# Expert rows added into out by accumulating scatters, gates made per group of rows

## The chip, the cores and the metric

One core of a Trainium2 chip runs the kernel. The engines are TensorE (PE), VectorE (DVE), ScalarE (ACT), GpSimd (POOL) and SyncE (SP); 16 DMA engines move data between HBM and the on-chip memories SBUF and PSUM. The metric is the device time of one execution in microseconds.

## The reference

x has 16 x 256 rows of 128 floats: T = 4096 rows, 32 tiles of 128. The first half is attention without softmax, which the kernel computes through small products per batch. The second half is a mixture of 8 experts, two for each row:

```
x = x + attention(layernorm(x)) @ Wo + bo       # 16 heads of 8, q and k of unit length
z = layernorm(x)
topk_w, topk_idx = top_k(softmax(z @ Wg.T), 2)
eo[e] = gelu(z @ w1[e] + b1[e]) @ w2[e] + b2[e]         # 128 -> 512 -> 128, erf gelu
x = x + sum over the two chosen experts of topk_w * eo[idx]
```

## The kernel before

T = 4096 rows are 8 groups (NG) of 4 tiles (G) of 128 rows. Each engine runs one program written out in order; they meet in semaphores.

**Attention stage.** All engines go through the same steps n of STEPS, each step working on several groups at different depths, in the order that the loop of each engine lists. For a group g: DVE takes statistics of x (stats_of_x, moments, squared, variance), ACT the root (deviation), DVE inverts (scale_and_shift), ACT makes xn (normalised), TensorE turns and projects it (turn_x, project), ACT squares q and k (squares), DVE sums (sums_of_squares), bounds (bounded), ACT takes the root (norms), DVE inverts (inverse_norms) and scales q and k (unit_qk). TensorE makes the rest of the attention (keys_of_x to attend). DVE adds it to x2, the rows after attention, which stay in SBUF (attended), finds the two largest logits and their experts (largest, where_largest, chosen, either), and from a running count the place of each row in its expert's region of xs (places). ACT writes the normalised rows twice into row (rows); GpSimd scatters them to xs, a table in HBM with one region for each expert, by 8 indirect DMAs of 128 rows for each group (line 463): 64 in all. SP hands row and slot back (s_free) two groups later. The weights w1 and w2 are split on the way into a high and a low part (centred_w1, high_w1, low_w1, high_w2, low_w2). weights() on DVE prepares the attention's weights once, in step -1.

After the last group DVE makes the tables of the slots (slot_table), SP and ACT write zero rows behind each expert's rows (pads), and DVE and ACT make all gates at once from the kept logits (lines 1068 to 1078 and 765).

**Slots.** There are NS = 71 slots of 128 rows of one expert each. For each, SP loads the rows from xs (line 396), U = 8 loads ahead at most, held back by s_back; TensorE turns them, multiplies by w1 in three products (lines 630 to 632), turns h and multiplies by w2 (lines 649 and 652); ACT does Gelu and the high parts, DVE the low parts (lines 1083 and 1088) and y (result, result_high, lines 1095 and 1100). GpSimd scatters y to ys (put, line 471), a table in HBM with a row for each of the two choices of each input row. The target row comes with the row from xs; rows of padding have a target outside of ys and are left out.

**Combining.** SP loads the two rows for each input row back from ys, group by group (line 405), DVE and ACT multiply by the gates and add to x2, ACT's queue writes out (lines 801 and 803).

## Time and profile before

| | us |
|---|---|
| median of 3 runs (323.61 to 323.96) | 323.89 |
| the profiled execution | 324.12 |
| its span, first to last instruction | 322.2 |

| engine | busy us | share of the span |
|---|---|---|
| PE | 254.3 | 79% |
| DVE | 208.9 | 65% |
| ACT | 170.3 | 53% |
| POOL | 149.9 | 47% |

The span in 40 slices of 8 us; a digit is the busy share in tenths, PEclk the granted TensorE clock, and DMA the mean busy share of the DMA engines:

```profile
PE   3847999998879530789999999999999999994000
PEld 1636777677558300269998999899899989893000
DVE  3474999799999679036556556655665666563475
ACT  4244566686754443055655655565565556551353
POOL 4380037757777778404443444444344444444000
PEclk9999997899995655699999999999999999999555
DMA  3798001111111114121221222222212222210996
```

The first 16 slices are the attention stage, then come the slots, and the last three are the combining stage. In the profile a name such as "ring<-xs" is output<-input, a group of instructions is named by its line in the kernel, "[0.30 <-issue]" is the idle time before an instruction and what ended it, and the time of a DMA "to landing" runs from its issue to the arrival of its semaphore.

### The profile page before, as it was taken

The page shows a single profiled execution, that of the slowest core. Times are in us where ns is not written, and L with a number is a line of the kernel's source. Part 1 is how long each engine was busy: PE and PEld are TensorE (multiplying, and loading weights), DVE is VectorE, ACT ScalarE, POOL GpSimd, SP SyncE. Part 2 cuts the span into 40 slices and gives each one's busy share as a digit, 9 for nine tenths or more (in the row PEclk, how much of TensorE's full clock was granted, in tenths as well). Part 3 has the DMA queues.
Part 4 walks back from the last instruction along what each step waited for, and adds up shares of the span by engine and source line. Part 5 has one row for each costly group of instructions (what it writes and reads, how often), then busy time and mean ns, then how long its engine had stood idle before and what let it go on. Part 6 is the DMA issues. An engine that isn't in the chain of part 4 may idle for free.

```text
span 322.2 us, 6689 instructions
## 1 busy us (share of the span) xinstructions
PE 254.3 (79%) x1611; PEld 211.2 (66%) x1611; DVE 208.9 (65%) x788; ACT 170.3 (53%) x392; POOL 149.9 (47%) x172
## 2 busy tenths in 40 slices
PE   3847999998879530789999999999999999994000
PEld 1636777677558300269998999899899989893000
DVE  3474999799999679036556556655665666563475
ACT  4244566686754443055655655565565556551353
POOL 4380037757777778404443444444344444444000
PEclk9999997899995655699999999999999999999555
DMA  3798001111111114121221222222212222210996
GB/s 86 219 356 238 2 16 50 58 36 57 52 49 49 50 49 100 51 50 51 57 68 53 59 67 66 60 55 67 65 48 67 63 59 60 63 43 1 257 337 188
DMA packets 33643, 27.60 MB, mean 86 GB/s; under 512 B 4395, under 2 KB 28601, under 8 KB 33607
## 3 DMA queue, kind: packets, MB, share of 16 engines
q1 hardware_dynamic: 24344, 16.39, 18.7%
q0 software_dynamic: 4320, 8.43, 7.9%
q10 hardware_dynamic: 4944, 2.36, 2.6%
q8 instruction: 16, 0.26, 0.4%
q14 instruction: 19, 0.16, 0.2%
HBM read 16.05 MB, written 11.57 MB: 86 GB/s over the span
## 4 chain that ended last, share of the span: by engine, by line
PE 55%; POOL 15%; DVE 10%; issue 7%; DMA 6%; ACT 3%; SPq 2%; DVEq 0%; POOLq 0%; ACTq 0%
POOL xs L463 15%; PE psQK L630 6%; PE psG L649 5%; PE psQK L632 5%; PE psQK L631 5%; PE psQ L639 5%; PE psO L649 5%; PE psKV L639 5%; PE psG L652 4%; PE psO L652 4%; DMA w1s<-ys 4%; PE psQK L519 3%; DVE n L896 2%; PE psO L624 1%; PE psX L624 1%
## 5 line engine op out<-in xcount | busy, mean ns | idle before, releaser
L471 POOL DMA_INDIRECT ys<-ring x71 | 68.9, 970 | 94.4 <-DVE ring L1100 92.4
L463 POOL DMA_INDIRECT xs<-row,slot x64 | 67.4, 1052 | 41.2 <-ACT row L689 22.2
L1088 DVE TENSOR_TENSOR hTl<-psQ,hTh 128x512 fp32r<-128x512 f32 x36 | 24.9, 692 | 29.2 <-ACT hTh L777 28.4
L785 ACT ACTIVATE ring<-psQK 128x512 f32<-128x512 f32 x71 | 42.9, 604 | 1.5 <-PE psQK L632 1.5
L1088 DVE TENSOR_TENSOR hTl<-psKV,hTh 128x512 fp32r<-128x512 f32 x35 | 24.2, 691 | 29.7 <-ACT hTh L777 29.7
L777 ACT CAST hTh<-psQ 128x512 fp32r<-128x512 f32 x36 | 21.1, 587 | 32.9 <-PE psQ L639 32.9
L777 ACT CAST hTh<-psKV 128x512 fp32r<-128x512 f32 x35 | 20.5, 587 | 30.3 <-PE psKV L639 30.3
L630 PE MATMUL psQK<-w1h,xTh 128*128 x71 | 34.2, 481 | 0.9 <-DVE xTl L1083 0.8
L632 PE MATMUL psQK<-w1h,xTl 128*128 x71 | 28.1, 395 | 0.0
L631 PE MATMUL psQK<-w1l,xTh 128*128 x71 | 28.0, 395 | 0.0
L649 PE MATMUL psO<-w2hl,hTh 128*128 x144 | 25.8, 302 | 0.6 <-DVE hTl L1088 0.6
L649 PE MATMUL psG<-w2hl,hTh 128*128 x140 | 25.1, 301 | 0.0
L639 PE MATMUL psQ<-ident,ring 128*128 128x128 f32 x144 | 21.7, 273 | 0.3 <-ACT ring L785 0.3
L639 PEld LDWEIGHTS psQ<-ident,ring 128*128 128x128 f32 x144 | 17.8, 140 | 5.5 <-ACT ring L785 0.8
L639 PE MATMUL psKV<-ident,ring 128*128 128x128 f32 x140 | 21.0, 272 | 0.1
L639 PEld LDWEIGHTS psKV<-ident,ring 128*128 128x128 f32 x140 | 17.3, 140 | 5.2 <-ACT ring L785 0.5
L652 PE MATMUL psO<-w2hl,hTl 128*128 x144 | 20.2, 262 | 0.0
L649 PEld LDWEIGHTS psO<-w2hl,hTh 128*128 128x128 f32 x144 | 19.5, 190 | 0.8 <-issue 0.8
L652 PE MATMUL psG<-w2hl,hTl 128*128 x140 | 19.6, 262 | 0.0
L519 PE MATMUL psQK<-wqk,xnT 128*128 128x256 f32 x64 | 19.0, 451 | 0.7 <-ACT xnT L697 0.7
L652 PEld LDWEIGHTS psO<-w2hl,hTl 128*128 128x128 f32 x144 | 19.0, 190 | 0.0
L649 PEld LDWEIGHTS psG<-w2hl,hTh 128*128 128x128 f32 x140 | 18.8, 190 | 0.0
(181 smaller groups left out, 577.1 us busy)
## 6 DMA issues: line engine op xcount, KB each, us to landing
ring<-xs SPq DMA_DIRECT2D x71, 64.5 KB, 1.9
w1s<-ys SPq DMA_DIRECT2D x16, 256.0 KB, 5.3
w1s<-in_L_ffn_w SPq DMA_DIRECT2D x1, 2048.0 KB
out<-x ACTq DMA_DIRECT2D x8, 256.0 KB, 4.8
ys<-ring POOLq DMA_INDIRECT x71, 2.2
xs<-row,slot POOLq DMA_INDIRECT x64, 2.4
xin<-in_L_attn_x SPq DMA_DIRECT2D x2, 256.0 KB, 3.4
b2bc<-in_L_ffn_b SPq DMA_DIRECT2D x1, 512.0 KB, 16.4
```

The source lines that it names most:

```text
L463: pool.indirect_dma_start(out=xs, out_offset=bass.IndirectOffsetOnAxis(ap=slot[:, p, j, k:k + 1], axis=0), in_=row[:, p, j, k, :], in_offs ...
L471: pool.indirect_dma_start(out=ys, out_offset=bass.IndirectOffsetOnAxis(ap=xt[:, b, D:ROW].bitcast(I32), axis=0), in_=y[:, b, :], in_offset ...
L519: mm = pe.matmul(psQK[:, j * 2 * D:(j + 1) * 2 * D], xnT[:, j, :], wqk[:], start=True, stop=True)
L630: pe.matmul(psH[q], xTh[:, q, :], w1h[:, bass.ds(e, 1), :], start=True, stop=False)
L631: pe.matmul(psH[q], xTh[:, q, :], w1l[:, bass.ds(e, 1), :], start=False, stop=False)
L632: pe.matmul(psH[q], xTl[:, q, :], w1h[:, bass.ds(e, 1), :], start=False, stop=True).then_inc(s_psH, 1)
L639: mm = pe.transpose(psHT[q][:, c * P:(c + 1) * P], h[:, q, c * P:(c + 1) * P], ident[:])
L649: pe.matmul(psY[q], hTh[:, q, at], w2hl[:, bass.ds(e, 1), w:w + 2 * D], start=c == 0, stop=False)
L652: mm = pe.matmul(psY[q][:, 0:D], hTl[:, q, at], w2hl[:, bass.ds(e, 1), w:w + D], start=False, stop=c == FC - 1)
L777: act.copy(hTh[:, b % 2], psHT[b % 2][:]).then_inc(s_hTh, 1)
L785: act.activation(h[:, b % 2, :], psH[b % 2], ACT.Gelu).then_inc(s_h, 1)
L1088: dve.tensor_tensor(hTl[:, b % 2], psHT[b % 2][:], hTh[:, b % 2].bitcast(F32), ALU.subtract).then_inc(s_hTl, 1)
```

## The change

- There is no ys. put scatters y into out itself with an addition in the DMA (compute_op add). Before that, SP writes x2 of each group to out in the attention stage (keep). out has 3 x 128 rows more, which take the rows of padding; the host cuts them off.
- Two scatters may touch the same row only when they belong to different experts. So put waits until the scatter two slots ahead has landed, and where the expert turned at the slot ahead (turn_table, ctab), for that one.
- A row in xs has one float more, its gate. Gates are made for each group on DVE and ACT (behind_largest, gap_of_logits, weights_of_experts, sum_of_experts, first_gate, second_gate), in the steps. DVE multiplies y by the gate in the slots (gated), which is a queue position behind low of a later slot.
- The combining stage and the gates after the last group are gone.
- Roots and reciprocals of the two norms are replaced by exp(-ln/2) on ACT and one step of refinement on DVE (Ln, Exp and for the norms of q and k also Square; four or five small operations on DVE: inverse_squared, inverse_error, inverse_refined, scaled_mean, shifted; norm_error, norms_refined). Ln and Exp are in one activation table, loaded first.
- w1 is centred in TensorE by one matrix (centre = ident + negmean), ACT and DVE read the result from PSUM, and DVE's addition for it (centred_w1) is gone. The parts of w2 are made three steps later, so that STEPS has two more.
- The orders of the loops on TensorE, ACT and DVE are new; weights() is now the first thing in its step. slots() holds what made slot and the target rows in places(), counted() what updated the counts.
- SP writes seven blocks of padding for unused slots instead of one, and the blocks behind the regions one by one between steps of the slot table.

```diff
-    ROW = D + 1
+    ROW = D + 2
...
-    out_v = out.rearrange("b (u p) f -> p (b u) f", p=P)
-    ys_v = ys.rearrange("(k t p) f -> p k t f", k=K, p=P)
+    out_v = out[0:T].rearrange("(t p) f -> p t f", p=P)
...
-            sp.wait_ge(s_zero, 2)
-            sp.dma_start(xs[E * REGION:E * REGION + P, :], padrow[:]).then_inc(s_pad, 16)
+            sp.wait_ge(s_zero, 4)
+            for j in range(NS - K * NT):
+                sp.dma_start(xs[E * REGION + j * P:E * REGION + (j + 1) * P, :], padslot[:, j % 2, :]).then_inc(s_pad, 16)
+            for j in range(3):
+                sp.dma_start(out[T + j * P:T + (j + 1) * P, :], padrow[:, 0:D]).then_inc(s_out, 16)
+
+            def keep(g):
+                sp.wait_ge(s_x2, g + 1)
+                sp.dma_start(out_v[:, g * G:(g + 1) * G, :], tiles_of(x2, g)).then_inc(s_out, 16)
 
...
+            keep(0)
+            keep(1)
             for n in range(NG - 2):
+                keep(n + 2)
                 sp.wait_ge(s_scat[n % 2], (n // 2 + 1) * (16 * G * K))
...
-            for c in range(NG):
-                if c >= R:
-                    sp.wait_ge(s_o, c - R + 1)
-                for k in range(K):
-                    sp.dma_start(yback[:, c % R, k], ys_v[:, k, c * G:(c + 1) * G, :]).then_inc(s_yb[c % R], 16)
...
-            def put(s, b, i, e):
+            pool.wait_ge(s_out, 16 * (NG + 3))
+            pool.wait_ge(s_ctab, 1)
+
+            def put(s, b, turned):
+
+                if 0 < s <= U:
+                    pool.wait_ge(s_back[(s - 1) % U], 16 * ((s - 1) // U + 1))
+                elif s > U:
+                    pool.wait_ge(s_back[(s - 1) % U], (turned & 16) + 16 * ((s - 1) // U))
+                    pool.sem_inc(s_turn, 1)
+                    pool.wait_ge(s_back[(s - 2) % U], 16 * ((s - 2) // U + 1))
                 pool.wait_ge(s_y, s + 1)
                 pool.indirect_dma_start(
-                    out=ys, out_offset=bass.IndirectOffsetOnAxis(ap=xt[:, b, D:ROW].bitcast(I32), axis=0),
-                    in_=y[:, b, :], in_offset=None,
-                    bounds_check=ys_bound, oob_is_err=False).then_inc(s_back[b], 16)
-            run_slots(put, pool)
...
+                    in_=y[:, b, :], in_offset=None, compute_op=ALU.add,
+                    bounds_check=out_bound, oob_is_err=True).then_inc(s_back[b], 16)
+
+            for i in range(NR):
+                v = pool.value_load(ctab[0:1, i:i + 1], min_val=0, max_val=16 * (2 ** U - 1)) if i else None
+                for b in range(U):
+                    if i * U + b < NS:
+                        put(i * U + b, b, (v >> b) if i else None)
...
-                    after(pe, s_w1, e)
-                    centred(psQ[:], w1s[:, e, :], b1row[0:1, e, :]).then_inc(s_psW, 1)
+                    pe.wait_ge(s_cf, 3)
+                    after(pe, s_w1l, e)
+                    pe.matmul(psQ[:], centre[:], w1s[:, e, :], start=True, stop=False)
+                    pe.matmul(psQ[:], onerow[:], b1row[0:1, e, :], start=False, stop=True).then_inc(s_psW, 1)
...
             for n in STEPS:
+                project(n)
+                values(n - 1)
+                turn_q(n - 1)
+                places(n - 2)
+                if n - 2 == NG - 1:
+                    count()
                 centre_w1(n - 2)
                 out_weights(n - 1)
                 turn_x(n + 1)
-                places(n - 2)
-                if n - 2 == NG - 1:
-                    count()
                 attend(n - 1)
                 share_of_x(n)
                 keys_of_x(n)
-                project(n + 1)
-                turn_q(n)
-                values(n)
...
-                after(pe, s_y, s - 1)
+                after(pe, s_yh, s - 1)
...
             for n in STEPS:
+                inverse_norms(n - 1)
+                squared_inverse(n - 1)
                 out_weights(n - 2)
                 rows(n - 3)
+                high_w1(n - 3)
                 turned_x(n)
                 keys(n - 1)
-                high_w2(n - 3)
-                high_w1(n - 4)
-                deviation(n - 1)
+                log_variance(n - 1)
+                inverse_deviation(n - 1)
                 squares(n)
+                high_w2(n - 4)
                 turned_q(n - 1)
                 normalised(n + 1)
-                norms(n)
-
-            pads(act, range(E // 2, E), s_pad2)
-
-            act.wait_ge(s_dlog, 1)
-            act.activation(dlog[:], dlog[:], ACT.Exp).then_inc(s_elog, 1)
+                log_norms(n)
+                weights_of_experts(n - 2)
+
+            act.wait_ge(s_ptab, 1)
+            for e in range(E // 2, E):
+                act.wait_ge(s_w1l, e)
+                pad(act, e, s_pad2)
...
-                dve.wait_ge(s_cf, 2)
+                dve.tensor_tensor(centre[:], ident[:], negmean[:], ALU.add).then_inc(s_cf, 1)
+                dve.wait_ge(s_cf, 3)
...
+            def first_gate(g):
+                if group(g):
+                    dve.wait_ge(s_exsum, g + 1)
+                    dve.wait_ge(s_free, g + 1)
+                    dve.reciprocal(row[:, g % 2, :, 0, D], exsum[:]).then_inc(s_gate0, 1)
+
+            def second_gate(g):
+                if group(g):
+                    dve.wait_ge(s_gate0, g + 1)
+                    dve.tensor_tensor(row[:, g % 2, :, 1, D], ex[:, :, 1], row[:, g % 2, :, 0, D],
+                                      ALU.mult).then_inc(s_gate, 1)
...
-            def centred_w1(e):
-                if 0 <= e < E:
-                    dve.wait_ge(s_psW, e + 1)
-                    dve.tensor_tensor(w1s[:, e, :], psQ[:], w1s[:, e, :], ALU.add).then_inc(s_w1, 1)
 
             def low_w1(e):
                 if 0 <= e < E:
                     dve.wait_ge(s_w1h, e + 1)
-                    dve.tensor_tensor(w1l[:, e, :], w1s[:, e, :], w1h[:, e, :].bitcast(F32),
+                    dve.tensor_tensor(w1l[:, e, :], psQ[:], w1h[:, e, :].bitcast(F32),
                                       ALU.subtract).then_inc(s_w1l, 1)
 
...
             for n in STEPS:
-                scale_and_shift(n - 1)
                 if n == -1:
                     weights()
                 share_of_x(n - 1)
-                as_float(n - 2)
+                low_w1(n - 3)
+                inverse_squared(n - 1)
+                chosen(n - 2)
+                inverse_error(n - 1)
+                either(n - 2)
+                inverse_refined(n - 1)
+                heads(n - 1)
                 share_and_bias(n - 1)
-                chosen(n - 2)
-                heads(n - 1)
-                either(n - 2)
+                scaled_mean(n - 1)
+                gap_of_logits(n - 2)
+                shifted(n - 1)
                 sums_of_squares(n)
+                places(n - 2)
+                bounded(n)
+                counted(n - 2)
                 stats_of_x(n + 2)
-                bounded(n)
-                inverse_norms(n)
-                places(n - 2)
+                sum_of_experts(n - 2)
+                slots(n - 2)
+                if n - 2 == NG - 1:
+                    slot_table()
+                low_w2(n - 8)
+                norm_error(n)
+                first_gate(n - 2)
+                norms_refined(n)
+                second_gate(n - 2)
+                if n - 2 == NG - 1:
+                    turn_table()
                 unit_qk(n)
+                logits(n - 1)
                 attended(n - 1)
                 largest(n - 1)
                 stats_of_x2(n - 1)
+                where_largest(n - 1)
                 moments(n)
-                centred_w1(n - 2)
+                as_float(n - 1)
                 squared(n)
-                low_w2(n - 5)
+                behind_largest(n - 1)
                 variance(n)
-                low_w1(n - 5)
-                where_largest(n - 1)
-                if n - 2 == NG - 1:
-                    slot_table()
...
+                dve.tensor_tensor(y[:, b, :], psY[b % 2][:, 0:D], y[:, b, :], ALU.add).then_inc(s_yh, 1)
+
+            def gated(s, b):
+                dve.wait_ge(s_yh, s + 1)
+                dve.tensor_scalar(y[:, b, :], y[:, b, :], xt[:, b, D:D + 1], None, ALU.mult).then_inc(s_y, 1)
...
                 low(s, b)
+                if not (static and s < 2):
+                    gated(s - 2, (b - 2) % U)
                 if not (static and s == 0):
                     result(s - 1, (b - 1) % U, i if b else i - 1, e[b])
                 if static and s == NS - 1:
                     result_high(s - 1, (b - 1) % U)
                     result(s, b, i, e[b + 1])
+                    gated(s - 1, (b - 1) % U)
                     result_high(s, b)
+                    gated(s, b)
             run_slots(one, dve, True)
```

## Rows read from the trace of the kernel before

**Rows 1.** table of stages: us, busy us and count by engine, TensorE clock, DMA share, GB/s

```profile
138.30:295.50 157.20, 154.79 (x1134) 139.53 (x1134) 92.25 (x282) 89.70 (x211) 67.95 (x71) 1.00 0.21 57
297.70:322.20 24.50, 0.00 (x0) 0.00 (x0) 14.47 (x40) 10.22 (x32) 0.00 (x0) 0.50 0.91 257
```

**Rows 2.** chain of waits in order of time: start us, us, what

```profile
295.47 2.08 DMA ys<-ring
...
299.23 4.54 DMA w1s<-ys
```

**Rows 3.** timeline of GpSimd: start us, us, engine, line, operation [idle before]

```profile
44.66 1.17 POOL L463 DMA_INDIRECT xs<-row,slot  x1 [20.07 <-ACT row L689]
...
67.16 0.97 POOL L463 DMA_INDIRECT xs<-row,slot  x1 [2.15 <-ACT row L689]
...
90.51 1.38 POOL L463 DMA_INDIRECT xs<-row,slot  x1 [0.30 <-issue]
...
123.88 4.15 POOL L463 DMA_INDIRECT xs<-row,slot  x1 [0.30 <-issue]
...
132.17 0.97 POOL L463 DMA_INDIRECT xs<-row,slot  x1 [0.30 <-issue]
...
144.71 0.97 POOL L471 DMA_INDIRECT ys<-ring  x1 [11.57 <-DVE ring L1100]
```

**Rows 4.** timeline of all engines where DVE and GpSimd overlap

```profile
84.09 0.97 POOL L463 DMA_INDIRECT xs<-row,slot  x1 [0.30 <-issue]
...
84.36 0.23 DVE L901 TENSOR_SCALAR n<-n 128x128 f32<-128x128 f32 x1
...
123.17 0.67 DVE L1006 TENSOR_TENSOR w2hl<-w2s,w2hl 128x512 fp32r<-128x512 f32 x1
...
127.21 0.43 DVE L1071 TENSOR_TENSOR xin<-xin,rall 128x256 f32<-128x256 f32 x1
```

**Rows 5.** the page's DMA issues: KB each, us to landing

```profile
ring<-xs SPq DMA_DIRECT2D x71, 64.5 KB, 1.9
...
ys<-ring POOLq DMA_INDIRECT x71, 2.2
```

**Rows 6.** timeline of the slots: the first load, and one slot

```profile
134.76 0.36 SPq L396 DMA_DIRECT2D ring<-xs  x1
...
201.70 0.69 DVE L1088 TENSOR_TENSOR hTl<-psQ,hTh 128x512 fp32r<-128x512 f32 x1 [0.85 <-ACT hTh L777]
...
202.51 0.28 DVE L1083 TENSOR_TENSOR xTl<-psO,xTh 128x128 fp32r<-128x128 f32 x1
...
203.26 0.97 POOL L471 DMA_INDIRECT ys<-ring  x1 [1.17 <-DVE ring L1100]
...
203.93 0.48 PE L630 MATMUL psQK<-w1h,xTh 128*128 x1
```

**Rows 7.** timeline of the first 24 us

```profile
7.58 0.16 DVE L888 SCALAR_TENSOR_TENSOR shift<-mms,rstd 128x4 f32<-128x4 f32 x1
...
11.31 1.09 PE L509 MATMUL psX<-ident,xn 128*128 128x128 f32 x4
...
11.67 0.28 DVE L839 TENSOR_SCALAR headmask<-headmask,mcol 128x128 f32<-128x128 f32 x1
...
17.19 7.39 POOL L450 TENSOR_TENSOR x<-xin,bobc 128x512 f32<-128x512 f32 x6 [5.91 <-DMA xin<-in_L_attn_x]
...
19.86 1.13 DVE L901 TENSOR_SCALAR n<-n 128x128 f32<-128x128 f32 x1
```

**Rows 8.** lines by form up to 135 us, DVE and ACT: busy us, mean ns

```profile
L906 DVE RECIPROCAL n<-nrm 128x128 f32<-128x128 f32 x8 | 7.6, 952 | 3.0 <-ACT nrm L732 3.0
...
L732 ACT ACTIVATE nrm<-n 128x128 f32<-128x128 f32 x8 | 2.5, 309 | 7.9 <-DVE n L901 7.9
```

**Rows 9.** timeline of DVE: sums of squares of two groups in a row

```profile
49.11 1.21 DVE L896 TENSOR_REDUCE n<-sq 128x128 f32<-128x1024 f32 x1
...
61.43 1.21 DVE L896 TENSOR_REDUCE n<-sq 128x128 f32<-128x1024 f32 x1
```

More of the change, by code:

```diff
@@ L294, in moe_block @@
         s_yl = sem("s_yl")
+        s_yh = sem("s_yh")
         s_y = sem("s_y")
         s_back = [sem(f"s_back{i}") for i in range(U)]
[L297 to L300 removed]
         s_out = sem("s_out")
@@ new lines, in scaled_mean, with shifted @@
+            def scaled_mean(n):
+                if norm(n):
+                    lo, hi, m = norm(n)
+                    dve.wait_ge(s_rstd, m)
+                    dve.scalar_tensor_tensor(out=shift[:, lo:hi], in0=sv[:, lo:hi, 0], scalar=-0.5, in1=rstd[:, lo:hi],
+                                             op0=ALU.mult, op1=ALU.mult).then_inc(s_sh, 1)
+            def shifted(n):
+                if norm(n):
+                    lo, hi, m = norm(n)
+                    if group(n + 2):
+                        dve.scalar_tensor_tensor(out=tiles_of(stdall, n + 2), in0=var[:, 0:G], scalar=1.0 / D,
+                                                 in1=rstd[:, 0:G], op0=ALU.mult, op1=ALU.mult)
+                    dve.wait_ge(s_sh, m)
+                    dve.tensor_scalar(shift[:, lo:hi], shift[:, lo:hi], 1.0, None, ALU.add).then_inc(s_shift, 1)
@@ L983, in places, with slots @@
                     dve.tensor_tensor(seen[:], seen[:], msum[:], ALU.add).then_inc(s_seen, 1)
+            def slots(g):
+                if group(g):
                     dve.wait_ge(s_sp, g + 1)
@@ L1036, in slot_table, with turn_table, chain @@
                     dve.tensor_reduce(ehalves, eshift[:], AX, ALU.add)
-                dve.tensor_scalar(rtab[:], rsum[:], float(E * REGION), None, ALU.min).then_inc(s_tab, 1)
+                dve.tensor_copy(rtab[:], rsum[:]).then_inc(s_tab, 1)
+            def turn_table():
+                links = [0]
+                def chain(ins):
+                    links[0] += 1
+                    ins.then_inc(s_gt, 1)
+                    dve.wait_ge(s_gt, links[0])
+                chain(dve.tensor_tensor(turns[:], etabf[0:1, 1:1 + NR * U], etabf[0:1, 0:NR * U], ALU.not_equal))
+                chain(dve.tensor_tensor(turns[:].rearrange("p (i j) -> p i j", j=U),
+                                        turns[:].rearrange("p (i j) -> p i j", j=U),
+                                        bits[:].unsqueeze(1).to_broadcast([1, NR, U]), ALU.mult))
+                with nc.allow_low_precision(reason="sums of powers of two below 2**12"):
+                    dve.tensor_reduce(ctab[:], turns[:].rearrange("p (i j) -> p i j", j=U), AX, ALU.add).then_inc(s_ctab, 1)
             for n in STEPS:
-                scale_and_shift(n - 1)
                 if n == -1:
```

246 lines of the change are left out of this document (140 added, 106 removed).

## The prediction

> **What bounds the kernel now.** I read the table of stages first, then the chain of waits, then the timelines of the stretches that the diff touches. The run has three stages. In the slots (138 to 295 us) TensorE is busy 98% of the time at full clock, and DVE and ACT 59% and 57%: TensorE sets the pace there [rows 1]. From 297.7 to 322.2 TensorE does nothing: this is the combining stage, DMA and DVE alone [rows 1]. The chain shows how it is entered: the last scatter into ys starts at 295.47, lands 2.08 us later, and only then the first load back begins, which takes another 4.54 us [rows 2]. The attention stage ahead of it all ends when GpSimd has issued its 64 scatters into xs: the first starts at 44.66, the last at 132.17, and one takes 0.97 us with 0.30 before it, 1.28 from start to start, with little else between them [rows 3]. So three questions decide: what the end costs without the combining stage, whether accumulating scatters keep up with the slots, and when the 64 scatters are through.
>
> **The end.** From the start of the last scatter to the end of the span lie 322.2 - 295.47 = 26.73 us, all of it removed but for one scatter's landing. Three things come in its place. The multiply by the gate is one DVE operation of 128x128 on SBUF; its nearest row took 0.23 us [rows 4]. It is queued so that the gates of slots 69 and 70 both come after the last product, so their scatters come close together; the second waits for its own y (+0.5 us) and for the issue of the one ahead (1.28 us spacing [rows 3]): the last scatter starts at about 296.8, +1.3. Its landing is no longer a plain write. A plain scatter lands in 2.2 us and a plain load of as many bytes in 1.9 us [rows 5]. An accumulating one has to read the old row before it writes: between 2.2 (the read hidden wholly) and 2.2 + 1.9 = 4.1 us (the read as a whole load ahead). I see no reason for less than 2.2. Most of a load's 1.9 us is start and completion, which one DMA pays once, so I take 3.2 us. With 0.2 us for the last wait the end is 1.3 + 3.2 + 0.2 = 4.7 us where it was 26.73: **-22.0 us**.
>
> **The slots.** Slots are (295.47 - 144.71) / 70 = 2.154 us apart (the first of the 71 scatters into ys starts at 144.71 [rows 3]). What is added on DVE is 0.23 us a slot. DVE waits before each subtraction of hTl (0.85 us at 201.70), the multiply comes behind it, and TensorE takes the xTl that is made from 202.51 to 202.79 only at 203.93 [rows 6]: the multiply delays xTl by 0.23 of 1.1 us of slack. Cost nothing; without that cover it would be 71 x 0.23 = 16 us. The psY buffer is handed back by the new semaphore s_yh at the same place as before. GpSimd gets a register load for each eight slots and two more waits for each slot; it sits idle 1.17 us a slot [rows 6], which covers them.
>
> New is that a scatter waits for the one two slots ahead to have landed (for the one just ahead where the expert turns). Queued behind that wait are all later scatters, and behind those the loads of the slots eight further on. With a landing L and 0.3 us of handover, two in flight need L + 0.3 <= 2 x 2.154 = 4.3, so L up to 4.0 costs nothing; at the 3.2 taken a turn of expert delays a scatter by 3.5 - 2.15 = 1.35 us, which is caught up again in about four slots. The loads tolerate it: from the issue of a slot's load (134.76 [rows 6]) to its scatter (144.71) and that one's landing are 12.1 us, eight slots are 17.2, and the gate and the longer landing take 2.3 of the 5.1 left. **0 us**, up to +17 at L = 4.1 (below). The 7 padded slots' rows are now written too; they were skipped. TensorE computes them either way.
>
> A rule of the Trainium skill speaks against the multiply. What the rows show: the 0.23 us operation at 84.36 ran in full inside a GpSimd scatter that had started at 84.09 [rows 3, 4]. The Trainium skill (SBUF — State Buffer, Who interferes with whom) says that a tensor_scalar on SBUF takes the port pair shared with GpSimd, and that the second to start blocks fully. By the rule the multiply could wait up to 0.97 us, which stays within the slack above; by the row nothing happens. The sum is the same but its margin isn't.
>
> **The attention stage, start.** weights() now comes ahead of the first group's norm on DVE. Before, shift was made at 7.58, ahead of it, and TensorE turned x at 11.31 [rows 7]. Now DVE starts the norm when weights() ends, at 11.67 + 0.28 = 11.95 [rows 7]; five dependent small operations at 0.2 us give 13.0, xn takes 1.65 us, so TensorE turns x at about 14.8: +3.5. Of that some comes back: GpSimd's additions for x2 (17.19 to 24.58) hold up DVE, so that n2's maximum took 1.13 us [rows 7] instead of 0.23 [rows 4], and a second operation soon after was held up likewise; shifted 3.5 us later most of that passes: 2 x 0.90 = 1.8 at best, I take -1.5 (0 to -1.8). In each early group the loop sums of squares, maximum, root, qk loses the four bn_stats (0.78 us, now behind the maximum), and has root and reciprocal (0.31 + 0.95 [rows 8]) replaced by three small activations and two small DVE operations (3 x 0.36 + 0.4): -0.55 for each of three groups, -1.7. Activations ahead of rows() on ACT: +0.6. First scatter +3.5 - 1.5 - 1.7 + 0.6 = +0.9 (-1 to +4).
>
> **Attention stage, pace.** The 64 scatters keep their 1.28 us; a row has one more element, no cost. DVE has to deliver a group each 10.2 us. From 67.16 to 123.88 lie 43 scatters, 1.32 us each or 10.55 per group [rows 3], and most groups began just when their rows were ready, so DVE took about as long. There w1's addition goes (0.67, of the shape of the row at 123.17 [rows 4]), the reciprocal goes (0.95 [rows 8]), w2's subtraction moves to later steps (0.67), and some ten small operations of 0.1 to 0.2 us come in (+1.5): about 9.8, just under GpSimd's 10.2, so GpSimd is the bound. It was starved once, by 2.15 - 0.30 us [rows 3]; I take half of that back: -0.9 (0 to -1.85).
>
> GpSimd also has longer scatters, 1.38 at 90.51 and like it in three more groups (1.31, 1.37 and 1.11 against 0.97), and one of 4.15 us at 123.88 [rows 3]. Each lies beside DVE subtractions of 128x512 with both inputs in SBUF (the lines L1000 and L1006); the long one spans eight such operations of that kind from 123.17 to 127.64, the first and the last shown [rows 4]. The subtraction for w1 now reads PSUM, and that for w2 moves to the end: the four smaller excesses go (0.41 + 0.34 + 0.40 + 0.14 = -1.3), and of the long one six subtractions 0.60 us apart are left, 3.6 us in place of 4.4: -0.8 (0 to -3.2, if they fall where no scatter is held).
>
> The writes of x2 to out (eight of 256 KB) are new in this stage, whose DMA share is one to two tenths; on SP they stand ahead of the s_free increments, which the wait for x2 precedes by a step: nothing. The seven fixed pad rows are written early, the eight others while the scatters of the last group run. ACT's two table loads at the end of the stage become one, ahead of 132: hidden. Sum: +0.9 - 0.9 - 1.3 - 0.8 = **-2.1 us**.
>
> **Sum.** 324.12 (the profiled execution; span 322.2 and 1.92 around it; the median is 323.89, 0.2 less) - 22.0 + 0 - 2.1 = **300.0 us**.
>
> **Rivals.** (1) The chain of scatters becomes the bound. At L = 4.1 a slot takes 4.4 / 2 = 2.2 us (+3.2 in 70), and each of seven turns leaves some 2 us that is not caught up (+14 to 15), less about 2 of buffer: +16, and +0.9 at the end: 317. It ends **slower than before** from about L = 4.4: (4.7 - 4.3) / 2 x 70 = 14, 7 turns 12, end 1.2, less 2, over 24. For it speaks that the landing is unmeasured and that descriptors of an addition may take longer to write than 0.97 us; against it, that a load in whole is 1.9 us. 9% for 305 to 323, 12% for slower. The Trainium skill (Collectives: The Full Stack, Why ReduceScatter is half of AllGather) says the DMA's own addition costs nothing but a second read, which halves its rate; that would leave L under 4. (2) The attention stage starves GpSimd. The step from 49.11 to 61.43 took 12.3 us [rows 9] (the page's clock line falls to 7 and 8 tenths there); with such steps for six or seven groups, (12.3 - 10.2) x 6.5 = +14: 314; half of it 307. 17% for 304 to 315. (3) The forecast with its bounds, 296 to 304: 62%.
>
> The range of 296 to 312 leaves out most of rival 1 and the far half of rival 2, some 18%. Faster by over 0.2% 0.87, within 0.2% (what a measurement of this kernel can tell from no change) 0.01, slower 0.12.
>
> **What the profile would show.** Right: no work of DVE or TensorE after 296 less the shift of the stage; scatters into out landing in 2.5 to 4.0 us and 2.15 us apart, TensorE 98% busy in the slots; first scatter into xs at 44 to 47, the last at about 130; no scatter of 1.3 us in the middle of the stage, and one of 3 us or more beside w2's subtractions. Wrong: landings over 4 us with GpSimd waiting on DMA and TensorE on loads; idle GpSimd between groups of eight; a first scatter past 48.

## The result and the profile after

The changed kernel takes 353.14 us (median of 4 runs, 350.67 to 355.7) where the kernel before took 323.92 beside it on the same chip: ratio 1.092, 95% interval 1.087 to 1.097. Forecast were 300.0 us, with a range of 296 to 312. The sign was wrong. Some executions of a kernel were more than 1.5% above its fastest; the medians and ratios of the table below leave them out. The profiled execution took 351.12 us, its span 349.4. The first lines are the 40 slices of the span (8.7 us each), busy share in tenths; then come rows of the costliest groups (count | busy us, mean ns | idle us before, and what ended it) and of the DMA issues (KB, us to landing).

```profile
PE   3458899999974307986699988888898798989770
DVE  2495899969996910454445556555565565555460
POOL 5380037776777783043465655564655746555573
PEclk9996999789998556999989999999999999999895
DMA  3898112212222312123234333343434333333332
...
L503 POOL DMA_INDIRECT out<-ring x71 | 109.8, 1547 | 99.5 <-DVE ring L1237 54.5
...
L666 PE MATMUL psX<-ident,ring 128*128 128x128 f32 x36 | 11.3, 314 | 14.5 <-DMA ring<-xs 14.2
...
ring<-xs SPq DMA_DIRECT2D x71, 65.0 KB, 1.9
out<-ring POOLq DMA_INDIRECT x71, 3.3
```

The combining stage of [rows 1] is gone: only 6.8 us lie between the start of the last scatter and the end of the span. But TensorE, full in the slots before, is now at 7 to 9 tenths there, and it waits for loads of x (L666). The table of stages says the same. Its columns are those of [rows 1]: the stretch and its length, then busy us and number of instructions of TensorE's products, of its weight loads, of VectorE, ScalarE and GpSimd, then the granted clock, the DMA share and GB/s:

```profile
178.00:330.00 152.00, 132.40 (x882) 113.41 (x881) 83.41 (x275) 72.04 (x165) 86.01 (x56) 0.99 0.39 50
```

TensorE does 132.4 us of work in 152 at full clock, and nothing else is near its limit: GpSimd 86, VectorE 83. So the time is in waits, not in an engine.

For all kernels of this study I read the starts of GpSimd's scatters from its timeline. "Step" is the mean distance of the first scatters of groups 1 to 8 into xs, "first 8" the mean interval of the first eight intervals of the 71 scatters into out (before: into ys), "rest" that of the other 62. After: (177.44 - 148.88) / 8 = 3.57 and (342.63 - 177.44) / 62 = 2.66. The experiments ran on three other chips; on each, the kernel before took 343.3 to 343.7 us, 20 more than on the chip of the forecast; the last of the experiments looks at where they go. So they are compared with runs of before of their own call, and by these columns.

| kernel | median us | ratio to before (95%) | first xs | step | first out | first 8 | rest | last out |
|---|---|---|---|---|---|---|---|---|
| before | 323.92 | | 44.66 | 10.70 | 144.71 | 2.17 | 2.15 | 295.47 |
| after | 353.14 | 1.092 (1.087 to 1.097) | 49.00 | 10.85 | 148.88 | 3.57 | 2.66 | 342.63 |
| before_again | 342.74 | 0.996 (0.991 to 1.001) | 44.70 | 13.27 | 163.52 | 2.17 | 2.15 | 314.27 |
| after_again | 379.94 | 1.109 (1.098 to 1.120) | 49.78 | 14.40 | 177.70 | 3.53 | 2.74 | 375.62 |
| x_freed | 350.53 | 1.019 (1.010 to 1.028) | 47.95 | 14.80 | 178.45 | 3.77 | 2.15 | 342.04 |
| gate_early | 362.80 | 1.059 (1.049 to 1.069) | 49.78 | 14.43 | 176.53 | 3.53 | 2.41 | 354.38 |
| plain_scatter | 362.14 | 1.058 (1.050 to 1.066) | 49.73 | 14.65 | 178.97 | 2.98 | 2.42 | 352.68 |
| first_pair | 372.81 | 1.089 (1.083 to 1.096) | 49.57 | 14.42 | 176.97 | 2.60 | 2.68 | 363.74 |
| freed_pair | 340.54 | 0.992 (0.989 to 0.995) | 47.60 | 14.63 | 176.49 | 2.65 | 2.15 | 331.07 |
| start_first | 379.00 | 1.101 (1.092 to 1.110) | 46.19 | 14.64 | 175.50 | 3.68 | 2.67 | 370.59 |
| all_slots | 337.71 | 0.982 (0.975 to 0.989) | 48.17 | 14.44 | 174.37 | 2.66 | 2.16 | 329.62 |
| centre_later | 357.88 | 1.043 (1.033 to 1.053) | 48.99 | 16.66 | 191.78 | 2.47 | 2.22 | 348.88 |
| centre_start | 357.57 | 1.044 (1.033 to 1.055) | 45.98 | 17.24 | 192.89 | 2.59 | 2.17 | 348.02 |

**Where the 51 us between 300.0 and 351.1 lie.** From the first scatter into out to the last: 193.75 us, where 70 x 2.154 + 1.3 = 152.1 were forecast: +41.7. Of that the first eight intervals hold 28.56 - 17.2 = 11.3, the other 62 hold 165.2 - 133.5 = 31.6, less the 1.3. The first scatter into out at 148.88, forecast at 144.71 - 2.1 = 142.6: +6.3. From the last one's start to the end of the span 6.8, forecast 3.4: +3.4. Around the span -0.2. The sum is 51.2.

**The loop.** The chain of waits shows where the slots' time goes. One round of it (start us, us, what):

```profile
291.76 3.36 DMA out<-ring
295.14 0.27 SPq L404
295.43 0.15 SPq L404
...
295.85 1.84 DMA ring<-xs
...
297.73 0.33 PE psX L666
...
300.78 0.29 DVE ring L1237
...
301.83 3.44 DMA out<-ring
```

By their places among the 71, the scatter at 291.76 is that of slot 50 and the one at 301.83 that of slot 54. The scatter of slot 50 lands after 3.36 us. SyncE then reads a row number (L404) and loads slot 58's x into the same buffer, for 0.71 + 1.84 us. TensorE turns it at 297.73, and 4.10 us later slot 54's scatter can start. The round is 10.07 us and takes the ring on by **four** slots: 2.52 us each, against TensorE's 2.15. The steps between turning slot 58 and scattering slot 54 stand in the timeline of after:

```profile
297.73 0.33 PE L666 MATMUL psX<-ident,ring 128*128 128x128 f32 x1 [1.56 <-DMA ring<-xs]
...
298.60 0.28 DVE L1233 TENSOR_TENSOR ring<-psO,ring 128x128 f32<-128x128 f32 x1
...
300.18 0.69 DVE L1221 TENSOR_TENSOR hTl<-psQ,hTh 128x512 fp32r<-128x512 f32 x1 [1.30 <-ACT hTh L845]
...
300.78 0.28 DVE L1237 TENSOR_SCALAR ring<-ring 128x128 f32<-128x128 f32 x1
...
301.83 1.55 POOL L503 DMA_INDIRECT out<-ring  x1 [2.69 <-DVE ring L1237]
```

VectorE's order ties them. Step 56 begins with turned_in(58), so all that follows waits for slot 58's x: result_high(54) at 298.60, low(56) at 300.18, and only then gated(54) at 300.78. In the kernel before, the scatter came right behind result_high (L1100 there); the same stretch of it, in the timeline of its second profile:

```profile
239.89 0.29 PE L624 MATMUL psX<-ident,ring 128*128 128x128 f32 x1
...
240.85 0.28 DVE L1100 TENSOR_TENSOR ring<-psO,ring 128x128 f32<-128x128 f32 x1
...
241.41 0.97 POOL L471 DMA_INDIRECT ys<-ring  x1 [1.18 <-DVE ring L1100]
```

Turning slot s + 4 to scattering slot s took 1.52 us there, 4.10 here. With the landing of 2.2 and the load of 1.9 of [rows 5] and the 0.71 for SyncE, before's round was 6.3 us in the 4 x 2.154 = 8.6 that TensorE gives it: hidden with 2.3 to spare. The change added 2.6 to this stretch (2.2 from the end of result_high(54) at 298.88 to the end of gated(54), the rest GpSimd's further waits) and 1.15 to the landing, 3.7 in all: 10.07, which is 1.45 over, or 0.36 a slot. The other 0.14 up to the 2.66 measured I didn't follow row by row. A part of it goes with the turns of expert: from slot 8 on, a scatter follows the one four slots ahead of it after 11.4 us on the mean where a turn lies between them, after 10.4 where none does.

### The profile page after: what moved, and what is told of

It reads as the page before. It is cut to its first block, busy times and chain, and to the rows that moved or that the text cites. A ratio compares the mean times of both kernels' runs of the same rounds, so it can differ in the third digit from the quotient of the medians.

```text
span 349.4 us, 7128 instructions
## 1 busy us (share of the span) xinstructions
PE 268.9 (77%) x1611; PEld 214.7 (61%) x1611; DVE 207.8 (59%) x864; ACT 165.7 (47%) x392; POOL 190.0 (54%) x183
## 4 chain that ended last, share of the span: by engine, by line
PE 35%; DMA 22%; issue 15%; POOL 10%; DVE 7%; ACT 5%; SPq 2%; POOLq 2%; DVEq 0%
DMA out<-ring 14%; DMA ring<-xs 6%; POOL out L503 5%; POOL xs L485 5%; PE psQK L556 4%; PE psQK L672 3%; PE psKV L574 2%; PE psQ L681 2%; PE psG L691 2%; PE psQ L660 2%; ACT xn L769 2%; PE psO L608 2%; PE psQK L673 2%; PE psQK L674 2%; PE psQ L631 2%
## 5 line engine op out<-in xcount | busy, mean ns | idle before, releaser
L503 POOL DMA_INDIRECT out<-ring x71 | 109.8, 1547 | 99.5 <-DVE ring L1237 54.5
L485 POOL DMA_INDIRECT xs<-row,slot x64 | 65.9, 1029 | 44.5 <-ACT row L732 24.4
L845 ACT CAST hTh<-psQ 128x512 fp32r<-128x512 f32 x36 | 21.1, 587 | 39.4 <-PE psQ L681 39.4
L672 PE MATMUL psQK<-w1h,xTh 128*128 x71 | 35.2, 496 | 3.4 <-DVE xTl L1216 0.9
L1216 DVE TENSOR_TENSOR xTl<-psX,xTh 128x128 fp32r<-128x128 f32 x36 | 10.4, 288 | 29.7 <-ACT xTh L840 29.2
L691 PE MATMUL psG<-w2hl,hTh 128*128 x140 | 25.8, 307 | 0.0
L840 ACT CAST xTh<-psX 128x128 fp32r<-128x128 f32 x36 | 9.6, 265 | 33.5 <-PE psX L666 33.4
L666 PE MATMUL psX<-ident,ring 128*128 128x128 f32 x36 | 11.3, 314 | 14.5 <-DMA ring<-xs 14.2
L681 PEld LDWEIGHTS psQ<-ident,ring 128*128 128x128 f32 x144 | 18.5, 145 | 5.8 <-ACT ring L853 0.8
L1237 DVE TENSOR_SCALAR ring<-ring 128x128 f32<-128x128 f32 x71 | 20.8, 292 | 0.0
L672 PEld LDWEIGHTS psQK<-w1h,xTh 128*128 128x128 f32 x71 | 14.3, 202 | 10.3 <-issue 10.0
```

The lines of the kernel that those rows point to most:

```text
L485: pool.indirect_dma_start(out=xs, out_offset=bass.IndirectOffsetOnAxis(ap=slot[:, p, j, k:k + 1], axis=0), in_=row[:, p, j, k, :], in_offs ...
L503: pool.indirect_dma_start(out=out, out_offset=bass.IndirectOffsetOnAxis(ap=xt[:, b, D + 1:ROW].bitcast(I32), axis=0), in_=y[:, b, :], in_o ...
L672: pe.matmul(psH[q], xTh[:, q, :], w1h[:, bass.ds(e, 1), :], start=True, stop=False)
L681: mm = pe.transpose(psHT[q][:, c * P:(c + 1) * P], h[:, q, c * P:(c + 1) * P], ident[:])
L691: pe.matmul(psY[q], hTh[:, q, at], w2hl[:, bass.ds(e, 1), w:w + 2 * D], start=c == 0, stop=False)
L845: act.copy(hTh[:, b % 2], psHT[b % 2][:]).then_inc(s_hTh, 1)
```

## The experiments

**x_freed: the loop is cut.** VectorE copies the row numbers aside, and SyncE's load waits for the gate's product instead of the scatter's landing.

```diff
-                after(sp, s_back[b], 16 * i)
+                after(sp, s_y, s - U + 1)
...
+                dve.tensor_copy(oidx[:, b:b + 1], xt[:, b, D + 1:ROW].bitcast(I32))
...
-                    out=out, out_offset=bass.IndirectOffsetOnAxis(ap=xt[:, b, D + 1:ROW].bitcast(I32), axis=0),
+                    out=out, out_offset=bass.IndirectOffsetOnAxis(ap=oidx[:, b:b + 1], axis=0),
```

> The changed kernel, where SP loads the x of slot s+8 as soon as y of slot s is multiplied, not when its scatter has landed: DVE copies the column of target rows to a small tile of its own just ahead of the multiply, and the scatter reads it there. The waits between scatters are as they were. Theory A: the loop is broken, the slots behind the first nine run at TensorE's 2.15 us, 318 to 324 us. Theory B: no change, 350 to 355.

The rest interval fell from 2.66 to 2.15, with the accumulating scatters, their waits and the late gate all in place. That is 0.51 x 62 = 31.6 us; the medians of x_freed and after_again lie 29.4 us apart. The first eight stayed (3.77). That 2.15 is also TensorE's pace is a coincidence, though. TensorE ends its last product at 329.79, and the last scatter starts 12.25 us later (in before 1.2 us, 294.28 and 295.47). From GpSimd's timeline of x_freed, the scatter at a turn of expert (slot 50), the next one and the last:

```profile
301.16 1.55 POOL L504 DMA_INDIRECT out<-ring,oidx  x1 [2.58 <-DMA out<-ring,oidx]
303.01 1.54 POOL L504 DMA_INDIRECT out<-ring,oidx  x1 [0.30 <-issue]
...
342.04 1.55 POOL L504 DMA_INDIRECT out<-ring,oidx  x1 [0.30 <-issue]
```

Of the 62 intervals of the rest, 47 are at most 1.90 us, which is GpSimd's 1.55 and 0.30 before it, and the six with a turn of expert take 4.13 to 5.14. So with the loop cut the chain of scatters runs almost without a gap: it sets this 2.15 itself, and it never caught up the first eight slots. TensorE no longer waits for loads. From the first scatter into out to the end of its last product lie 151.3 us, in before 149.6, in after 190.4.

**gate_early: the gate goes ahead of low.** One call is moved in VectorE's loop.

```diff
                     result_high(s - 2, (b - 2) % U)
+                    gated(s - 2, (b - 2) % U)
                 low(s, b)
-                if not (static and s < 2):
-                    gated(s - 2, (b - 2) % U)
```

> The changed kernel with one edit: DVE multiplies y by the gate right behind result_high, ahead of low, instead of behind it. Theory A (the ring of eight x buffers closes a loop: a scatter's landing 3.35 us, SP 0.7, the load 1.85, then TensorE, ACT and DVE until y is multiplied, about 10.1 us in the trace from 291.76 to 301.83, and the y that waits for it is only four slots on, so 2.5 us a slot): the multiply no longer waits for the transposes, hTh and low of a later slot, the loop loses about 1.6 us, the pace behind the first nine slots falls from 2.66 to 2.2 to 2.3 us and the time from 353 to 325 to 333 us. Theory B (the waits of a scatter for the two ahead of it are the bound themselves): the multiply's place is off the chain, no change, 350 to 355.

Rest 2.41: 0.25 less a slot, 1.0 less a round, of some 1.9 that lay between result_high and gated. The place of a 0.28 us operation cost 0.25 x 62 = 15.5 us. Forecast were 1.6 less a round and 2.2 to 2.3 us a slot, so this one fell short; the turns, which take 4.06 to 4.77 us here too, weren't in that forecast.

**plain_scatter: no addition.** compute_op is left out, so rows are overwritten and out holds only the last contribution of each; all waits stay.

> The changed kernel without the addition in the DMA: scatters into out overwrite, so the sum over the two experts and x2 is left out of the result; all waits and places are as they were. Both theories: GpSimd's 1.55 us goes back to 0.97 and the landing from 3.3 to 2.2 us. A: loop 10.1 - 1.1 = 9.0 us or 2.25 us a slot, and the first eight intervals, which wait for each other, 2.5 instead of 3.57: together 353 - 25 - 8 = 318 to 324. B: the same sign, with the pace at TensorE's 2.15 and 314 to 318.

```profile
L503 POOL DMA_INDIRECT out<-ring x71 | 68.9, 971 | 119.6 <-DVE ring L1237 83.5
```

GpSimd is busy 0.97 us for each where the accumulating one took 1.55, and rest is 2.42, again about 1.0 less a round, of which the landing (2.2 against 3.3) is the whole. So gate and landing share the excess, and taking away either alone leaves the pace over 2.15. Both forecasts missed: A had 2.25 and 2.5 for the first eight, B had 2.15, and measured were 2.42 and 2.98. The addition is one part of the loop's length; x_freed, which keeps it, shows that TensorE is held by it only through the ring.

**first_pair: the first eight slots.** The code holds each of slots 1 to 8 to the landing of the one just ahead, whether or not the expert turned. Here eight small transfers give each s_back a first 16, and the table decides for these slots too.

```diff
+            for b in range(U):
+                pool.dma_start(dum[:, b:b + 1], padrow[:, 0:1]).then_inc(s_back[b], 16)
...
-                if 0 < s <= U:
-                    pool.wait_ge(s_back[(s - 1) % U], 16 * ((s - 1) // U + 1))
-                elif s > U:
-                    pool.wait_ge(s_back[(s - 1) % U], (turned & 16) + 16 * ((s - 1) // U))
+                if s > 0:
+                    pool.wait_ge(s_back[(s - 1) % U], (turned & 16) + 16 * ((s - 1) // U + 1))
...
```

> The changed kernel with the first eight scatters held to the rule of the later ones (wait for the one two ahead, and for the one just ahead only where the expert turned) instead of always waiting for the one just ahead. Eight small DMAs into a spare tile give the semaphores their first value while GpSimd is idle. The first eight intervals, 3.57 us, fall to 2.15 to 2.6 us: 8 x 1.0 to 1.4 = 8 to 11 us, so 342 to 345, if the later pace of 2.66 does not change. If the lag of the first eight was what held the later slots back, more: 330.

First eight 2.60 instead of 3.57, 7.8 us in all; rest unchanged at 2.68. The median is 7.1 us below after_again's.

**after_again and freed_pair: both causes together.** after_again is the changed kernel once more; freed_pair is x_freed and first_pair together.

> The changed kernel once more, on the chip of the other runs of this call. Theory A (loop through the x ring, set by DMA landings): first eight out scatters 3.5 to 3.6 us apart, the rest 2.6 to 2.7, whatever the attention stage takes on this chip; ratio to before 1.08 to 1.12. Theory B (the slots slowed down because TensorE's clock fell or the engines are in each other's way): the interval would move with the chip.

> The x buffer is freed by VectorE's last read (indices copied aside) and the first eight slots follow the pair rule through eight small transfers that give each semaphore a first 16. Theory A: with the loop through the ring cut, first eight at 2.2 to 2.6 us (was 3.57), the rest at 2.15 (was 2.66): 31 + 8 to 11 us less than after_again, so some 10 to 14 us below before on the same chip if the attention stage is not longer than that of before. Rival (accumulating scatters themselves are the chain: landing 3.3 us for each pair plus 1.55 us): the first eight stay at 2.6 and the rest can't come below 2.4.

after_again gave 3.53 and 2.74 though its attention stage took 29 us more: the intervals hardly follow the chip (start_first and first_pair have 2.67 and 2.68). freed_pair is 379.94 - 340.54 = 39.4 us shorter, with first eight 2.65 and rest 2.15. From its first scatter into out to the last it takes 154.6 us where after took 193.75: 39.2 of the 41.7 us that the forecast had missed. TensorE is full again (table of stages of freed_pair):

```profile
200.00:320.00 120.00, 119.89 (x883) 108.59 (x882) 85.98 (x332) 70.05 (x164) 84.62 (x56) 1.00 0.46 61
```

GpSimd has little to spare even here. TensorE's last product ends at 324.81 and the last scatter starts 6.3 us later, in before 1.2. The turns of expert take 4.03 us and more, 5.71 at the one among the first eight, and each slot behind one wins back 2.15 - 1.85 = 0.30 us at most. The expectation of 10 to 14 us below before had a condition, an attention stage no longer than before's; the first scatter into out came 13 us later than in before_again, and 0.8% are left.

**start_first: the first norm ahead of weights().** The five small operations of the first norm's inverse root run before weights() in VectorE's step -1; no operation is added or lost.

```diff
                 if n == -1:
+                    for part in (inverse_squared, inverse_error, inverse_refined, scaled_mean, shifted):
+                        part(-2)
                     weights()
```

> The five small VectorE operations of the first norm's inverse square root go ahead of the preparation of the weights; nothing else changes. If the late first xs scatter (49.0 us against 44.7) comes from these operations standing behind weights() and then being held 1.1 us each beside GpSimd's long one, the first xs scatter comes 2 to 4 us earlier than in after_again and the whole kernel is 2 to 4 us shorter (ratio to after_again 0.99). If the rival holds (the first groups are bound by loads and by the new order of TensorE's steps), under 1 us moves. The slots' intervals stay 3.57 and 2.66.

The first scatter into xs came at 46.19 instead of 49.78, -3.6 us. On the time nothing is shown: the medians differ by 0.9 us, and the ratios' intervals (1.098 to 1.120 and 1.092 to 1.110) overlap. The 3.6 us are not clear either, since x_freed and freed_pair, with nothing changed there, came at 47.95 and 47.60. The rows show what was lost there in after; from its timeline:

```profile
13.25 0.17 DVE L968 TENSOR_SCALAR shift<-shift 128x4 f32<-128x4 f32 x1
...
15.24 1.09 PE L546 MATMUL psX<-ident,xn 128*128 128x128 f32 x4 [3.51 <-ACT xn L769]
...
17.18 7.37 POOL L471 TENSOR_TENSOR x<-xin,bobc 128x512 f32<-128x512 f32 x6 [5.83 <-DMA xin<-in_L_attn_x]
17.33 1.14 DVE L938 TENSOR_TENSOR rsq<-rs 128x4 f32<-128x4 f32 x1 [2.46 <-ACT rs L752]
18.50 1.19 DVE L944 SCALAR_TENSOR_TENSOR rsq<-var,rsq 128x4 f32<-128x4 f32 x1
19.72 1.19 DVE L951 SCALAR_TENSOR_TENSOR rstd<-rsq,rs 128x4 f32<-128x4 f32 x1
20.94 1.19 DVE L958 SCALAR_TENSOR_TENSOR shift<-sv,rstd 128x4 f32<-128x4 f32 x1
...
22.16 1.19 DVE L968 TENSOR_SCALAR shift<-shift 128x4 f32<-128x4 f32 x1
```

The second group's norm now meets GpSimd's additions: five dependent operations take 1.14 to 1.19 us each instead of 0.16. In start_first they run at 15.86 to 16.65, ahead of GpSimd's start at 17.21, in 0.15 to 0.17 us each.

**all_slots: freed_pair, gate_early and start_first together.**

> freed_pair, with y's second half made right behind its first, ahead of low(s), and with start_first's order. Theory A: the same intervals as freed_pair (2.15, TensorE's pace, which neither place of y changes), so only start_first's 2 to 4 us come off freed_pair. If y's place costs by itself (VectorE's order delays the x rest for the next product), the rest interval rises above 2.15, to 2.2 to 2.4, and this kernel is slower than freed_pair by 3 to 15 us less the start's gain.

337.71 us, 0.982 of before (0.975 to 0.989): only this one and freed_pair (0.992, 0.989 to 0.995) lie below before with their whole interval, by under 2%. Rest is 2.16, so the gate's place costs nothing once the loop is cut, and saves nothing either. The first scatter into xs came at 48.17, not earlier than freed_pair's 47.60: the start's gain didn't show here, and the 2.8 us between the medians lie within the intervals' overlap.

**before_again, centre_later, centre_start: the attention stage on these chips.** Its steps are 14.4 to 14.8 us in the changed kernels there, 10.85 on the first chip. before_again is the kernel before with a profile of its own. centre_later moves two products of TensorE in freed_pair, centre_start adds start_first's order.

```diff
-                centre_w1(n - 2)
                 out_weights(n - 1)
                 turn_x(n + 1)
+                centre_w1(n - 2)
```

> The kernel before once more, with a profile of its own on this chip. Groups of xs scatters of the changed kernel stand 15 us apart on this chip instead of 10.4. Theory P (TensorE, at a lower granted clock, is the bound of an attention step in any order of the steps): before shows steps of 13 to 15.5 us too, with granted clock 0.7 or less in the middle of the stage, and 20 us more than in its first profile. Theory O (the new order of the steps, with the two long w1 products between the counting products and the output weights, makes a chain that is only hidden at full clock): before stays at 10.5 to 12.5 us a step at the same clock.

> freed_pair with one move on TensorE: the two products that centre one expert's w1 go behind turn_x instead of between places and out_weights. Theory O: steps of the attention stage fall from 15.3 us by the 2 to 4 us for which VectorE's pos and TensorE's out_weights wait there, 8 to 25 us less in all than freed_pair (ratio to before 0.92 to 0.97). Theory P: TensorE has the same work and is the bound, so the steps stay within 0.5 us of 15.3 and the ratio at freed_pair's 0.992 within 0.01.

> centre_later with start_first's order of the first norm. The start's gain of 2 to 4 us adds up with whatever centre_later shows: ratio to before 0.006 to 0.012 below centre_later's.

The kernel before has steps of 13.27 us there. The same stretch of its two profiles, first chip above (columns as in [rows 1]; the last three are granted clock, DMA share, GB/s):

```profile
50.00:80.00 30.00, 27.29 (x157) 22.04 (x158) 26.54 (x127) 20.61 (x46) 21.45 (x23) 0.89 0.15 50
```

```profile
50.00:80.00 30.00, 24.52 (x111) 19.65 (x110) 19.44 (x99) 15.92 (x36) 17.76 (x19) 0.72 0.12 41
```

So a lower granted clock goes with before's 20 us on these chips, and the changed kernels take 1.1 to 1.5 us a step more than before there, 0.15 on the first chip. centre_later was meant to take that back. It did the opposite: steps of 16.66 us, 17 us more in all; an order that was to take 8 to 25 us off. The waits of TensorE from 50 to 150 us in centre_later begin with this row (us in total, times, longest):

```profile
PE psG L604 <- DVE pos L1099: 31.1, 6, 6.9
```

In freed_pair (50 to 160 us) that row reads 10.4 us in 3 times. Between counting (places) and out_weights TensorE has to wait for VectorE's pos, since both products lie in one PSUM bank, and the two products for w1 were the work that filled this wait. Theory P falls as well: TensorE has the same work in both kernels, and if its work were the bound, moving it could not add 2 us a step. The wait above says that the bound of a step in centre_later is a chain through TensorE and VectorE. Which link of it made after's steps longer than before's wasn't settled. centre_start repeats centre_later (357.57) and shows no gain from the start, though its first scatter came at 45.98 instead of 48.99.

## Why the prediction was wrong

**The end: a term too small.** The combining stage went as forecast. 20.0 us came off behind the last scatter's start instead of 23.3 (26.73 less 3.4). The landing was 3.3 us, forecast 3.2. But the span ends 6.8 us after the last scatter starts, so 3.5 us follow the landing, where I had 0.2. They belong to GpSimd's DRAIN, its last instruction but the closing semaphores (after, then before; ns, and the start in us):

```profile
L58 POOLq DRAIN  x1: 7074/7074/7074, 342.1 to 342.1; - x1
```

```profile
L60 POOLq DRAIN  x1: 7728/7728/7728, 295.2 to 295.2; - x1
```

In after it lasts from 342.1 to 349.1, and the span ends at 349.4. In the kernel before it was as long, but the combining stage hid it: it could have been read there. With plain scatters, which land in 2.2, the drain took 8.2 us and the stretch from the last scatter's start 7.7 (352.68 to 360.4), so it isn't the landing that sets the end. What makes the drain as long as it is wasn't tested.

**The slots: the step that failed** is "the loads tolerate it: from the issue of a slot's load (134.76) to its scatter (144.71) and that one's landing are 12.1 us, eight slots are 17.2". Three things in it were wrong. First, the latency was read from slot 0, which ran through an empty pipeline: from turning its x (136.68) to its scatter (144.71) 8.03 us. In steady state the kernel before took 10.0 to 10.4, because the turning of slot s + 4 stands ahead of slot s's result; the loop closes after four slots, not eight. Second, the gate was entered with its duration of 0.23 us, "queued behind low" was written down in the change and not carried into the sum: low waits for TensorE's products of a later slot, and the move cost 2.2 us of latency with the operation. Third, SyncE's 0.7 us of reading a row number and issuing was left out. 1.9 + 10.3 + 2.2 for the gate + 3.3 + 0.7 make 18.4 us, more than 17.2; by the steady rows of before the loop would have been seen to close. (The 2.3 us entered for the gate and the longer landing aren't the sum of the prediction's own 0.23 and 3.2 - 2.2, which is 1.2.) gate_early and plain_scatter show a part each, 1.0 us a round; in x_freed TensorE waits for no load.

**The first eight slots: a line that was not costed.** The prediction said that a scatter waits for the one just ahead where the expert turns. The code does so for slots 1 to 8 in any case, at 3.3 us of landing and some 0.25 of handover for each. first_pair took 7.8 of the 11.3 us back; one of its eight intervals holds a turn of expert (4.12 us).

**Rival 1 had the right sign with the wrong mechanism.** It was to need a landing over 4.4 us; the landing was 3.3, and two in flight need 3.3 + 0.3 <= 4.3, as computed. In freed_pair TensorE keeps its pace with these same waits. But the chain of scatters has less to spare than the prediction gave it: it left out GpSimd's own 1.55 us (it had 0.97 and 1.28 from start to start, measured 1.85), and had 3.5 us for a turn, which takes 4.03 or more. Without the loop this shows: freed_pair's last scatter lags 5 us more behind TensorE than before's, and in x_freed the scatters set the pace behind the first eight slots. The slower outcome came from a loop that none of the cases named, and so its chance of 12% was worked out from the wrong quantity; that the sign agreed was luck.

**The attention stage.** First scatter forecast +0.9 (-1 to +4), measured +4.3. The late weights() cost 3.9 on TensorE's first turn (forecast 3.5; an operation more, centre, had been left out). What failed is the "-1.5" for the overlap with GpSimd's additions: it did not pass but grew, from two operations held up to five. The pace from first to last scatter came out at 84.9 us for 87.5, -2.6, forecast -3.0: GpSimd's spacing was the bound on that chip, the excesses in the middle were 0.1 and 0.2 us, and the long scatter beside w2's subtractions was there as forecast (its 3.55 us below). Of the 6.3 us by which the first scatter into out was late, 3.4 are the start, 0.4 the pace, and 2.4 lie behind the last scatter into xs: there slot 0 took 10.0 us from its turning (138.88) to its scatter, not 8.03, again because the gate stands behind the low of a later slot.

```profile
118.00 1.55 POOL L485 DMA_INDIRECT xs<-row,slot  x1 [0.30 <-issue]
...
121.12 3.55 POOL L485 DMA_INDIRECT xs<-row,slot  x1 [0.30 <-issue]
```

```profile
120.14 3.68 DVE L1124 TENSOR_TENSOR w2hl<-w2s,w2hl 128x512 fp32r<-128x512 f32 x6
```

**The rule on the shared port.** The gate's product took 0.28 us at 300.78 with GpSimd idle, and 0.29 on the mean of 71 (20.8 us busy). 41 of the 71 ran at the same time as an accumulating scatter of 1.55 us; these took 0.31 us on the mean and 0.59 at most, the other 30 took 0.28. By the rule that the prediction quotes from the Trainium skill (SBUF — State Buffer, Who interferes with whom), the second to start blocks fully, and so it could have waited up to 1.55 us: the trace doesn't show that. That section also says that a VectorE instruction with two SBUF inputs contends with a GpSimd instruction that reads SBUF. The five small operations above, each held about as long as one of GpSimd's six additions (7.37 / 6 = 1.23 us), agree with it, and so does the scatter of 3.55 us beside six back-to-back subtractions, if its row numbers are what it reads from SBUF. The product by itself moved nothing in the sum.

**The read ahead of the write** (the Trainium skill, Collectives: The Full Stack, Why ReduceScatter is half of AllGather). The landing grew by 1.1 us for a second read, less than a load's 1.9, which agrees. GpSimd's own part grew too, by 0.58 us a scatter (0.97 to 1.55).

## What to carry to other kernels

When a change lengthens the time until a buffer comes free, follow the loop back to the same buffer in steady state and count the slots by which it advances, not the buffers of the ring; the first slot's latency is that of an empty pipeline. An operation added in an engine's queue costs the latency of what it is queued behind, here 2.2 us for a 0.28 us product. If a wait only guards a few words of a buffer (here the row numbers of a scatter), copying them aside frees the buffer early: 0.15 us a slot on an engine with time to spare took 29 us off. And where a pace comes out equal to that of the engine that was the bound, look at whether that engine's last work and the chain's end together: in x_freed they lie 12 us apart.

## What the runs showed of the hardware

- An indirect scatter of 128 rows of 512 bytes with addition keeps GpSimd for 1.55 us and lands 3.3 us after its start; without it, 0.97 and 2.2. From start to start the closest are 1.85 and 1.27 us.
- GpSimd's DRAIN at the end of the kernel took 7.1 us in after, 7.3 in freed_pair, 8.2 in plain_scatter and 7.7 in before. In the three whose last DMA is GpSimd's, the span ends 0.2 to 0.3 us after it; in before the combining stage hid it.
- The kernel before took 324 us on one chip and 343 to 344 on three others. From the first scatter into ys to the end of the span the two profiles of before take 177.5 and 177.3 us (322.2 - 144.71 and 340.8 - 163.52); all of the difference lies ahead of it, in the attention stage, where TensorE's granted clock was 0.72 instead of 0.89 from 50 to 80 us. A change judged on one chip can have another ratio on the next: 1.092 and 1.109 for this one.
- Five small VectorE operations of 128x4 took 1.14 to 1.19 us instead of 0.16 while GpSimd added two SBUF tensors of 128x512, each one anew; a sixth, between them, took 0.15.
